# Normalisations and gates on GpSimd, and the last third of the keys loaded feature-major

## The reference, cut to what matters

```python
# x (16, 100, 128), ctx (16, 1444, 128), all fp32; mask (16, 1444) is 0 or 1
att = (n1 @ w_input.T) + (n1 * dot_scale) @ ctx.T - 1e30 * mask[:, None, :]   # n1 = layernorm(x)
x = x + tanh(g_xattn) * softmax(att) @ ctx
# 8 experts, the two best per token; F = 512; gates are the two softmax values, scaled to sum 1
n2 = layernorm(x)
gates, idx = top_k(softmax(n2 @ w_router.T), 2)
y_e = (silu(n2 @ w_gate[e].T) * (n2 @ w_up[e].T)) @ w_down[e].T
x = x + tanh(g_ffn) * sum over both experts of gate * y_e
```

## Time and profile before

| what | value |
|---|---|
| median of 3 runs | 318.53 us (317.22 to 320.13) |
| the profiled execution, its own time | 320.17 us |
| its span | 318.4 us |
| PE busy | 252.2 us (79%) |
| DVE, ACT, POOL busy | 159.5, 122.7, 118.1 us (50, 39, 37%) |
| moved by DMA | 39.27 MB, mean 123 GB/s |
| chain that ended last | PE 51%, DVE 16%, DMA 10%, POOL 10%, issue 7% |

### The profile page before, as it was taken

One profiled execution on the slowest core, in us unless ns is written; L12 is line 12 of the kernel. 1 busy time (PEld: TensorE's weight loads), 2 busy tenths in 40 slices (PEclk: granted clock), 3 DMA queues, 4 the chain that ended last, 5 costly groups with the idle time before them and its releaser, 6 DMA issues.

```text
span 318.4 us, 5672 instructions
## 1 busy us (share of the span) xinstructions
PE 252.2 (79%) x1556; PEld 206.9 (65%) x1557; DVE 159.5 (50%) x522; ACT 122.7 (39%) x275; POOL 118.1 (37%) x173
## 2 busy tenths in 40 slices
PE   0865999999899869976679439980999999999920
PEld 0435777777777748774649427860888888788710
DVE  2444666787767656663676313682234333342305
ACT  1133355554455523551314004440355545455400
POOL 2240433344145555557215716353132332323230
PEclk9996899999799998979696676996699999999975
DMA  5987677877488883997000113112211111114027
GB/s 116 237 207 200 158 202 196 202 200 193 112 197 213 227 209 88 240 272 247 33 0 9 32 39 91 40 33 71 59 47 47 52 33 50 42 41 144 20 54 280
DMA packets 21246, 39.27 MB, mean 123 GB/s; under 512 B 3830, under 2 KB 14134, under 8 KB 21222
## 3 DMA queue, kind: packets, MB, share of 16 engines
q1 hardware_dynamic: 17366, 34.38, 41.1%
q0 software_dynamic: 2560, 3.77, 4.1%
q10 hardware_dynamic: 1296, 0.83, 0.8%
HBM read 32.87 MB, written 6.09 MB: 122 GB/s over the span
## 4 chain that ended last, share of the span: by engine, by line
PE 51%; DVE 16%; DMA 10%; POOL 10%; issue 7%; ACT 2%; SPq 2%; DVEq 0%; POOLq 0%
PE psum L1094 8%; PE psum L997 7%; PE psum L977 6%; PE psum L1072 6%; POOL slots L494 6%; PE psum L965 5%; PE psum L1074 5%; PE psum L1073 5%; DMA x_all<-in_x 5%; PE psum L1083 4%; DVE scores L720 3%; PE psum L987 3%; DVE ctxT L683 2%; DMA mask_scaled<-scores 2%; PE psum L1062 1%
## 5 line engine op out<-in xcount | busy, mean ns | idle before, releaser
L540 POOL DMA_INDIRECT results<-y_sb,dest x32 | 31.1, 971 | 71.1 <-DVE dest L904 49.4
L997 PE MATMUL psum<-ctx_sb,probsT 120*100 120x128 f32 (+1 forms) x384 | 54.1, 306 | 0.0
L997 PEld LDWEIGHTS psum<-ctx_sb,probsT 120*100 120x100 f32 (+1 forms) x384 | 51.4, 195 | 0.0
L977 PE MATMUL psum<-ctxT,qT 128*100 128x512 f32 (+1 forms) x96 | 43.7, 593 | 2.7 <-DVE ctxT L683 2.7
L907 DVE SCALAR_TENSOR_TENSOR scores<-probs,row_in,psum 128x512 f32<-128x512 f32 x32 | 23.9, 747 | 41.9 <-ACT probs L635 41.9
L484 POOL TENSOR_TENSOR w_lo<-w_raw,w_hi 128x512 fp32r<-128x512 f32 x16 | 20.4, 1276 | 49.5 <-ACT w_hi L592 49.5
L494 POOL DMA_INDIRECT slots<-pair_rows,slot_i x32 | 33.0, 1030 | 9.3 <-issue 9.3
L1094 PE MATMUL psum<-w_down,hidT 128*128 x256 | 35.0, 281 | 1.0 <-ACT y_sb L645 0.6
L635 ACT ACTIVATE probs<-psum 128x512 f32<-128x512 f32 x32 | 19.1, 597 | 42.8 <-PE psum L1074 42.8
L1094 PEld LDWEIGHTS psum<-w_down,hidT 128*128 128x128 f32 x256 | 32.0, 197 | 1.7 <-issue 1.7
L1072 PE MATMUL psum<-w_hi,rowT_hi 128*128 x64 | 29.9, 467 | 3.3 <-DVE scores L907 2.3
(11 more groups left out here) (125 smaller groups left out, 355.5 us busy)
## 6 DMA issues: line engine op xcount, KB each, us to landing
ctx_sb<-in_ctx SPq DMA_DIRECT2D x16, 720.0 KB
maskb<-mask_scaled SPq DMA_DIRECT2D x16, 564.1 KB
w_raw<-in_w_experts SPq DMA_DIRECT2D x16, 256.0 KB, 9.3
row_in<-slots SPq DMA_DIRECT2D x32, 65.0 KB, 1.8
w_down<-in_w_experts SPq DMA_DIRECT2D x4, 512.0 KB, 9.8
x<-x_all SPq DMA_DIRECT2D x2, 400.0 KB
ctx_sb<-x SPq DMA_DIRECT2D x1, 800.0 KB, 4.9
ctx_sb<-results SPq DMA_DIRECT2D x4, 200.0 KB, 4.0
```

The source lines that it names most:

```text
L540: nc.gpsimd.indirect_dma_start(results, bass.IndirectOffsetOnAxis(ap=dest[:, s:s + 1], axis=0), y_sb[:, s, :], None).then_inc(y_stored[s], 16)
L977: last = nc.tensor.matmul(scores_ps[0:Q, n:n + m], qT[:, b % 2, :], ctxT[:, n:n + m], start=True, stop=True)
L997: last = nc.tensor.matmul(attn_ps[0:Q, 0:D], probsT[0:rows[c], c, :], ctx_sb[0:rows[c], b % RING, c, :], start=(c == 0), stop=(c == CHUNKS ...
```

## The change

- The third group of keys (480 of 1444) is no longer transposed on PE. The host gives it feature-major as `ctx_t`, SP loads it into `third` (two buffers, 240 KB a batch), and DVE evicts it from there into ctxT. ACT evicts both other groups.
- Both normalisations move from DVE to POOL. The second writes straight to `pair_rows`, so `copy_pairs` is gone, and PE transposes from `pair_rows`.
- The gates are computed on POOL in `gates(p)` (six operations, chained by waits), `place` keeps the rows only. `ratios` is gone.
- Parts are of 4, 4, 3, 3, 2 batches for 4, 4, 4, 2, 2. EARLY is 10 for 11. Choosing a part is one piece in step 5, 9, 12, 15; ranks and placing follow in step 6, 10, 13, 16. `tile_tables` is split in `tile_runs` and `tile_tables`. The last part's pieces stand one or two tile steps earlier.
- POOL scatters one or two batches per step, behind `normalise2`.
- PE transposes xn2 behind the keys, and `attend` is split around `route`. ACT has a dummy Exp at its start.
- SP's order gets `load_third(b+2)` between mask and weights, and the loads of x stand earlier.

```diff
-PARTS = [(0, 4), (4, 8), (8, 12), (12, 14), (14, 16)]
+PARTS = [(0, 4), (4, 8), (8, 11), (11, 14), (14, 16)]
-EARLY = 11
+EARLY = 10
+    OWN = GROUPS - 1
+        third = sb("third", [P, 2, K - group_start[OWN]])
...
+            def load_third(b):
+                sp.dma_start(third[:, b % 2, :], ctx_t[b, :, :]).then_inc(third_loaded[b % 2], 16)
...
             for b in range(B - 2):
                 sp.wait_ge(scores_done, b + 1)
                 load_mask(b + 2)
+                sp.wait_ge(ctxT_dve, b + 1)
+                load_third(b + 2)
                 load_weights(b + 2)
                 if b + RING < B:
                     sp.wait_ge(attn_raw, b + 1)
...
+            def normalise2(b):
+                s = b % 2
+                pool.wait_ge(rstd2_done, b + 1)
+                nc.gpsimd.tensor_scalar(pair_rows[:, b, :, 0:D], x_all[:, b, :].unsqueeze(1).to_broadcast([Q, 2, D]),
+                                        mv2[:, s, 0:1], rstd2[:, s:s + 1], ALU.subtract, ALU.mult).then_inc(xn2_done, 1)
...
+            def gates(p):
+
+                b0, b1 = PARTS[p]
+                n = b1 - b0
+                pool.wait_ge(gap_done, p + 1)
+                if p == 0:
+                    pool.wait_ge(tanh_done, 1)
+                chain(nc.gpsimd.tensor_tensor(ratio[:, 0:n], euler[:, 0:n], gap[:, 0:n], ALU.pow))
+                chain(nc.gpsimd.tensor_scalar(den[:, 0:n], ratio[:, 0:n], 1.0, None, ALU.add))
+                chain(nc.gpsimd.tensor_tensor(gate1[:, 0:n], den[:, 0:n], minus[:, 0:n], ALU.pow))
+                chain(nc.gpsimd.tensor_scalar(gate1[:, 0:n], gate1[:, 0:n], tanh_g[0:Q, 1:2], None, ALU.mult))
+                nc.gpsimd.tensor_copy(pair_rows[:, b0:b1, 0, D], gate1[:, 0:n])
+                nc.gpsimd.tensor_tensor(pair_rows[:, b0:b1, 1, D], gate1[:, 0:n], ratio[:, 0:n], ALU.mult).then_inc(gates_done, 1)
+                pool.wait_ge(gates_done, p + 1)
...
+            SCATTERS = {7: (0, 1), 8: (1, 2), 9: (2, 3), 10: (3, 4), 11: (4, 6), 12: (6, 7), 13: (7, 8), 14: (8, 10), 15: (10, 11)}
             for b in range(B + 1):
+                if b >= 2:
+                    root2(b - 2)
+                    normalise2(b - 2)
+                if b in (7, 11, 14):
+                    pool.wait_ge(placed, {7: 1, 11: 2, 14: 3}[b])
+                for t in range(*SCATTERS.get(b, (0, 0))):
+                    scatter(t)
+                if b < B:
+                    split_weights(b)
...
+                if b + 2 < B:
+                    normalise1(b + 2)
+                if b in (5, 9, 12, 15):
+                    gates({5: 0, 9: 1, 12: 2, 15: 3}[b])
...
+            def evict_ctxT(b):
+                dve.wait_ge(third_loaded[b % 2], 16 * (b // 2 + 1))
+                wait(dve, scores_raw, b)
+                apart(dve)
+                nc.vector.tensor_scalar(ctxT[:, group_start[OWN]:K], third[:, b % 2, :],
                                         ds_col[:, 0:1], wi_col[:, 0:1], ALU.mult, ALU.add).then_inc(ctxT_dve, 1)
...
             def between(n):
-                if n == 1:
+                if n == 0:
                     copy_logits(B - 1)
                     choose_first(LAST)
+                if n == 1:
+                    choose_second(LAST)
                 if n == 2:
-                    choose_second(LAST)
-                if n == 4:
                     copy_rank(LAST)
                     place(LAST)
-                if n == 5:
+                if n == 3:
+                    tile_runs(True)
+                if n == 4:
                     tile_tables(True)
...
                 if n == 0:
                     transpose_xn2(B - 1)
                 if n == 1:
-                    route(B - 1)
-                if n == 3:
                     ranks(LAST, B)
```

More of the change, by code:

```diff
@@ L136, in build @@
         rstd2 = sb("rstd2", [Q, 2])
-        xn2 = sb("xn2", [Q, 2, D])
+        warm = sb("warm", [P, 1])
         xn2T = sb("xn2T", [P, Q])
@@ L213, in build @@
         mask_stored = sem("mask_stored")
+        third_loaded = [sem(f"third_loaded{s}") for s in range(2)]
         mask_loaded = [sem(f"mask_loaded{s}") for s in range(2)]
@@ L501, in _ @@
             root1(0, 1)
+            normalise1(0)
             link(nc.gpsimd.memset(empty[:, :], 0.0))
@@ L567, in _, with evict_ctxT @@
             act.dma_start(wr_sb[:, :], w_router).then_inc(small_loaded, 16)
-            def ctxT_first(b):
-                act.wait_ge(ctxT_raw, b * GROUPS + 1)
-                nc.scalar.activation(ctxT[:, 0:group_start[1]], ring_ps[0][:, 0:group_start[1]],
+            def evict_ctxT(b, g):
+                act.wait_ge(ctxT_raw, b * OWN + g + 1)
+                at, end = group_start[g], group_start[g + 1]
+                nc.scalar.activation(ctxT[:, at:end], ring_ps[g][:, 0:end - at],
                                      ACT.Identity, bias=wi_col[:, 0:1], scale=ds_col[:, 0:1]).then_inc(ctxT_act, 1)
@@ L614, in _ @@
             act.wait_ge(scale_loaded, 32)
+            nc.scalar.activation(warm[:, :], wi_col[:, :], ACT.Exp)
             copy_qT(0)
-            ctxT_first(0)
+            evict_ctxT(0, 0)
+            evict_ctxT(0, 1)
             act.wait_ge(small_loaded, 48)
@@ L705, in statistics2 @@
                 nc.vector.bn_aggr(mv2[:, s, :], stats2[:, s, :]).then_inc(mv2_done, 1)
-            def normalise2(b):
-                o = b % 2
-                dve.wait_ge(rstd2_done, b + 1)
-                wait(dve, pairs_done, b - 1)
-                nc.vector.tensor_scalar(xn2[:, o, :], x_all[:, b, :], mv2[:, o, 0:1], rstd2[:, o:o + 1],
-                                        ALU.subtract, ALU.mult).then_inc(xn2_done, 1)
             def masked_max(b):
@@ L823, in tile_tables @@
                 link(nc.vector.tensor_tensor(jump[:, :], origin[:, 1:E + 1], origin[:, 0:E], ALU.subtract))
+                if late:
+                    link(nc.vector.tensor_tensor(tail_row[:, :], count, region[:, 0:E], ALU.add))
+            def tile_tables(late):
+                nt = LATE if late else EARLY
+                t0 = EARLY if late else 0
                 link(nc.vector.tensor_tensor(reached[:, 0:nt, :], tile_f[:, 0:nt, :],
@@ L841, in step @@
                     statistics2(b - 2)
-                if b + 1 < B:
-                    normalise1(b + 1)
                 if 0 <= b - 1 < B:
                     attention_gain(b - 1)
-                if 0 <= b - 2 < B:
-                    normalise2(b - 2)
                 if b < B:
                     masked_max(b)
-                if b == 7 or b == 11:
-                    copy_rank((b - 7) // 4)
-                if b == 14 or b == 16:
-                    copy_rank(b // 2 - 5)
+                if b in (6, 10, 13, 16):
+                    copy_rank({6: 0, 10: 1, 13: 2, 16: 3}[b])
                 if b + 1 < B:
-                    ctxT_rest(b + 1, 1)
-                    ctxT_rest(b + 1, 2)
-                if b < 2:
-                    statistics1(2 * b + 4)
-                    statistics1(2 * b + 5)
-                if 8 <= b + 6 < B:
+                    evict_ctxT(b + 1)
+                if b == 1:
+                    for t in range(4, 8):
+                        statistics1(t)
+                if 2 <= b and b + 6 < B:
                     statistics1(b + 6)
@@ L887, in _ @@
                 step(b)
+            residual(B - 1)
+            statistics2(B - 1)
             def rowT_low(i, k):
@@ L931, in _ @@
             rowT_low(0, 0)
-            residual(B - 1)
-            statistics2(B - 1)
-            normalise2(B - 1)
             over_tiles(dve, tile_step, between)
@@ L952, in transpose_ctx @@
                 pe.wait_ge(ctx_loaded[s], 32 * (b // RING + 1))
-                for g in range(GROUPS):
+                for g in range(OWN):
                     if b == 0:
@@ L989, in transpose_probs, with attend @@
                     last.then_inc(probsT_raw, 1)
-            def attend(b):
+            def attend(b, first_group, last_group):
                 wait(pe, x2_done, b)
-                for g in range(GROUPS):
+                for g in range(first_group, last_group):
                     pe.wait_ge(probsT_done, b * GROUPS + g + 1)
@@ L1100, in tile_step @@
                     transpose_rows(i, k + 1)
+                if k == 1:
+                    route(B - 1)
                 if k == EARLY:
@@ L1143 @@
         "ctx": a["ctx_1024"],
+        "ctx_t": a["ctx_1024"][:, order[sum(rows[:2 * GROUP]):], :].transpose(0, 2, 1),
         "mask": mask[:, order],
```

164 lines of the change are left out of this document (64 added, 100 removed).

## The result

| | before | changed |
|---|---|---|
| median | 319.33 us (4 runs) | 342.62 us (342.16 to 345.65, 4 runs) |
| ratio | 1 | 1.0751, 95% interval 1.0656 to 1.0847 |
| profiled execution, its span | 320.17, 318.4 | 342.26, 340.3 |
| S(2), S(15) | 35.3, 160.9 | 40.0, 182.4 |
| first tile's row, row 8 | 189.1, 221.8 | 209.1, 241.5 |

The change makes the kernel 7.5% slower, where 317.5 us and at most 327 were predicted. The page of the changed kernel: busy time of the engines, then the costliest lines of its chain, two groups (busy, mean ns of one, idle before and its releaser), and two DMA issues with KB and the median us to landing.

The account below looks back on a forecast made before the run. PE was taken as the bound, busy 7.94 of 8.00 us in a quiet step, with waits for POOL. Terms +7.8, -6.9 and -1.8 us took 320.17 to 319.3, by the median 317.5 us; range 306 to 327.

Parts of the forecast that it names:

- A step behind a wait: Batch phase: a step whose score waited for the third, clock loss included, takes 9.0 us; 7.5 without a wait.
- The routing step: Steps 6, 10, 13: PE waits for xn2 behind DVE's choices and POOL's gates, so such a step takes 11.6 us.
- (b): Rival for the batch phase: the third is never late, steps of 8.0, routing steps 9.5, 296 us; chance 0.17.
- X: Batch phase: least time from attend's end to the score needing the third issued then, 10.3 us, 9.6 of it landing.
- The chain of steps: Batch phase: start and step lengths added up put the start of score(15) at 168.7, 7.8 us later than before.
- 1.5 us of clock per wait: Batch phase: after each 2.8 us wait for the third PE runs at lower clock and loses 1.5 us.
- (c): Rival: slower, the clock doesn't return within a step, each wait costs 2.7 us, 325 us; chance 0.23 including POOL still late.
- (a): Rival: waits of 2.8 us don't cost clock, or the third lands earlier; 313, 312 by the median; chance 0.20.
- normalise2 "writes the 256 elements that the copy writes in 0.40, and I take 0.6": Second normalisation, moved to POOL: 0.4 to 0.8 us, taken as 0.6 from a copy of the same size.
- S(15) to the first row, 21.3: From the start of score(15) to the first tile's row: 21.3 us for 28.2 before, a gain of 6.9.
- route(13) is done at +6.1: In the stretch before the tiles: routing of batch 13 ends 6.1 us after the start of score(15).
- Tiles, "some 1.8 us sooner": In the tiles: late_ready, and row 8 with it, come some 1.8 us sooner; bounds 0 and 7.4.

Follow-up runs that it names:

- e2: The changed kernel with the third loaded for batches 0 and 1 only, so later scores use wrong keys: 317.56 us, ratio 0.989.
- e3: The changed kernel without the third's load; PE transposes all 12 key chunks, DVE evicts the last group from PSUM: 316.56 us, ratio 0.989.
- e7: e3 with normalise2 on POOL writing 128 columns, signalling, then copying them: 314.77 us, ratio 0.981.
- e10: e7 with the last part's gates and scatters one tile sooner on POOL: 311.78 us, ratio 0.975.
- e5: e3 plus the changed kernel's loads of the third, into a buffer that nothing reads: 322.75 us, ratio 1.003.
- e12: e10 with the tables on DVE moved ahead of the wait for logits: 309.45 us, ratio 0.969.

## Why the prediction was wrong

**What held.** The bound of the old kernel, and the new wait, its place, and that it comes every second step. A step behind a wait was put at 9.0; 59.50 to 68.64 is 9.1. The routing step at 81.08 is 11.9 for 11.6. That the rest of the change is a gain held in sign.

**Where most of the miss lies.** The prediction puts a price on both halves of the change: rival (b), in which the third is never late, is at 296, and the forecast at 317.5. So the late third was to cost 21.5 us; it costs 25.1 (the changed kernel against e2). The other half was to give 22.5 us, from 318.5 to 296; without the late third the kernel takes 317.6 (e2) or 316.6 (e3), 1% less than before. That step, the gain of 22.5 us from all that isn't the third, failed by some 21 us. Waits for scatter lumps went, and waits for normalise2, the gates and DVE's choices came in their place (in e3 1.6 us for xn2 in steps 6 and 10, 3.8 and 4.1 us for xn2 and passed behind S(15)). In e3 the first row comes 8.4 us sooner than before, but from there to the end it takes 134.4 us for 129.3, while the prediction had 1.8 less. In the changed kernel the waits for the third hide a part of these others (1.0 us for xn2 in step 6), so that step by step the miss divides otherwise.

**What failed, step by step**, from 319.3 to the 342.3 of the profiled execution, 23 us:

- *X, "The third stands exactly where w_raw stood": 10.3.* From the end of attend to S(n+2) it is 11.4, 12.4, 11.2, 10.7 and 11.4 in the waits of S(4) to S(12): 5.6 us over five pairs, and S(2) is 1.1 late. The chain of steps, moreover, adds 10.2 and not 10.3 per pair, 0.5 in all. The row was right for the old queue. With the third in it, w_raw itself lands after 10.5 us for 9.3 on the whole page: I added a transfer to the queue and kept the landing time of the queue without it.
- *1.5 us of clock per wait.* Right at S(4) (1.46 in the scores). Scores of 5.10 and 5.11 us for 2.59 behind waits of 4.61 and 3.34 lose 2.5, rival (c)'s side; those behind 2.87 lose nothing, (a)'s side. Over the five waits the scores lose 8.2 us for 7.5, so the term was right in the mean, but the length of a wait alone does not give its price. The trace before had said so, where the prediction has no wait between none and 2.2: behind 1.43 us PE took 2.27 and 3.56 us for 1.43 and 2.85. Steps 8, 10, 12 and 13 are 1.7, 1.7, 0.9 and 2.2 longer than the sum had them. In 10 and 13 that is not the clock alone:
- *normalise2 "writes the 256 elements that the copy writes in 0.40, and I take 0.6".* It takes 1.24 us, normalise1 0.83 for half. PE waits for it up to 3.4 us, 10.5 in all. The bounds of 0.4 to 0.8 came from a copy, and don't hold the value. The same normalisation of 100x128 took DVE 0.35 us before. The term's whole effect is small: e7 takes back 0.43 per step and gains some 2 us.
- *S(15) to the first row, 21.3.* It is 26.7. "route(13) is done at +6.1" is at +11. The eleven operations of tile_runs stand on DVE ahead of residual(13), which I had left out of this sum, and one of them takes ten times as long as it should (last section); POOL idles 2.28 us for DVE there. The rest isn't theirs: POOL's four scatters and w_lo end only at 184.75, normalise2 is longer, and at the low clock the two parts of attend take 3.63 and 2.01 us for 1.91 and 1.10. Behind that come the choices, root2 and normalise2 again, and the granted clock of the stretch is 0.68.
- *Tiles, "some 1.8 us sooner".* They take 1.9 longer from the first row to the end. Row 8 is only 0.3 sooner behind the first row (32.4 for 32.7): PE stands 2.7 us at the ranks, and POOL's scatters wait until 234.1 behind the results of two tiles, though the slots were there at 228.0. I had counted late_ready's work and not POOL's order. e10 bears it out: one tile sooner on POOL gives 3.0 us by the medians (the intervals of e7 and e10 overlap slightly). The other 2.2 us lie behind row 8, 1.4 of them in the tiles up to the last row; no run separates them.

X, the clock and normalise2 are in the 13.7 us up to S(15) (7.2 are X with the start and the 0.5, 6.5 the longer steps), the tail is 5.4 and the tiles 3.7: 22.8 of 23. The wait of 1.43 us in the trace before, and what follows it:

```profile
80.83 0.30 PE L1004 MATMUL psum<-identity,xn 100*128 100x100 f32 x1 [1.43 <-DVE rank_sb L775]
80.97 2.27 PE L965 MATMUL psum<-identity,ctx_sb 121*128 121x121 f32 x12
...
83.27 3.56 PE L997 MATMUL psum<-ctx_sb,probsT 121*100 121x128 f32 x24
```

In the changed kernel, root2(13) on POOL, PE at the last part's ranks in the tiles, and POOL's late scatter:

```profile
187.03 0.24 POOL L457 TENSOR_SCALAR var<-mv 100x1 f32<-100x1 f32 x1 [2.28 <-DVE mv L736]
```

```profile
221.42 0.33 PE L1031 MATMUL psum<-chosen,before 100*100 100x24 f32 x2 [2.71 <-DVE passed L789]
```

```profile
234.10 1.02 POOL L531 DMA_INDIRECT slots<-pair_rows,slot_i  x1 [0.30 <-issue]
```

**The rivals.** (b), the third never late, was put at 296. In e2 and e5 nothing waits for it, and they give 317.6 and 322.8. So even a right guess on the third would have missed: in e3 the routing steps take 11.2 to 12.4 us for (b)'s 9.5, and the tail 25.9 for 21.3. (c) had the sign, and its mechanism in two of five waits, but put 325. (a) had one wait of five for it, and the third landed later, not earlier. The range failed as a whole because its ends came from one term each, while five terms missed to the same side: the third's landing, POOL's price, POOL's order and DVE's order were all taken too cheap, and a late engine makes the next one later.

## What to carry over

A new transfer on a full queue doesn't land after the old time of its neighbour. Take the bytes that will be ahead of it, and its own, at the rate of the busy stretch, as a lower bound (here 7.8 us of 9.9), and compare with the lead that its trigger gives; if that is short, issue it a step earlier or move it ahead of the large transfers that have more time (here worth some 5 to 6% by one move) before anything else. Ask also who lands later then, and whether the saved work was on the path at all: e2 saved 0.4 us a step on PE and gained nothing. When work moves to another engine, write down that engine's whole queue between two handovers; e10 and e12 together gained 1.7% by the medians, 1.3% by the ratios, through nothing but the place of small operations.
